# The last 48 rows of two expert tiles' down products, as four 64x64 products side by side

## The reference

```python
DIM = 256; INTER = 176; N_EXPERTS = 16; TOP_K = 2; N_SHARED = 2

def _swiglu(t, wa, wb, wo):
    h = jax.nn.silu(t @ wa.T) * (t @ wb.T)
    return h @ wo.T

t = x.reshape(-1, DIM)                       # 2048 tokens
scores = jax.nn.softmax(t @ gate_w.T, axis=-1)
weights, indices = jax.lax.top_k(scores, TOP_K)
y = jnp.zeros_like(t)
for e in range(N_EXPERTS):
    w_e = jnp.sum(jnp.where(indices == e, weights, 0.0), axis=-1)
    y = y + _swiglu(t, w1[e], w3[e], w2[e]) * w_e[:, None]
z = _swiglu(t, sw1, sw3, sw2)                # the shared experts, inner size 352
return (y + z).reshape(shape)
```

## Time and profile before

| | us |
|---|---|
| median of 3 runs | 681.43 |
| profiled execution | 684.4 |
| its span | 682.6 |
| PE busy | 608.7 (89%) |
| DVE busy | 527.3 (77%) |
| ACT busy | 517.4 (76%) |
| POOL busy | 427.4 (63%) |
| L1476, up products of the expert tiles, each column half | 59.5 and 59.6 |
| L1142, staging of down weights, 40 | 23.1 |

### The profile page before, as it was taken

The page is one execution under the profiler, slowest core; times in us unless marked ns, Lnnn a source line. Parts: engine busy times, 40 slices in busy tenths (PEclk is TensorE's granted clock), DMA queues, the critical chain, the costliest instruction groups (busy, mean ns, idle before and its releaser), DMA issues.

```text
span 682.6 us, 12684 instructions
## 1 busy us (share of the span) xinstructions
PE 608.7 (89%) x4476; PEld 498.8 (73%) x4479; DVE 527.3 (77%) x899; ACT 517.4 (76%) x1182; POOL 427.4 (63%) x261
## 2 busy tenths in 40 slices
PE   5799999999994698899999999899998787879993
PEld 3388999999993445799999999887774443445662
DVE  6898999999997899899999999878534543444464
ACT  3999999999995988999999999865454442333435
POOL 0028999999997004799999999920224465455402
PEclk8979999999996999999999999999999988898997
DMA  7022333333320000344444444461111122122163
GB/s 191 6 64 82 111 112 112 111 103 111 111 82 1 1 4 21 103 153 153 155 148 150 152 154 154 137 202 61 56 48 61 63 73 83 63 77 64 54 262 123
DMA packets 41595, 67.76 MB, mean 99 GB/s; under 512 B 6688, under 2 KB 20928, under 8 KB 41536
## 3 DMA queue, kind: packets, MB, share of 16 engines
q1 hardware_dynamic: 37696, 56.50, 25.7%
q0 software_dynamic: 3840, 10.49, 4.8%
HBM read 57.28 MB, written 9.70 MB: 98 GB/s over the span
## 4 chain that ended last, share of the span: by engine, by line
ACT 44%; PE 24%; DVE 12%; POOL 11%; issue 3%; another core or an unknown queue 2%; DMA 2%; DVEq 1%; POOLq 0%; ACTq 0%; SPq 0%
ACT rings L1045 20%; POOL arena L1184 9%; PE both L1476 8%; ACT rings L1033 8%; ACT late L1033 8%; PE bank L1483 4%; PE both L1463 4%; DVE st L443 1%; POOL residual L1194 1%; ACT tok_a L923 1%; ACT rings L923 1%; PE bank L1584 1%; ACT tok_a L996 1%; DVE rings L866 1%
## 5 line engine op out<-in xcount | busy, mean ns | idle before, releaser
L1184 POOL TENSOR_TENSOR arena<-arena,rings 128x1024 f32<-128x1024 f32 x126 | 296.3, 2372 | 13.3 <-DVE arena L658 8.7
L1383 PE MATMUL both<-rings,tok_a 128*128 128x128 f32 x1152 | 171.7, 278 | 3.7 <-DVE arena L658 2.9
L1383 PEld LDWEIGHTS both<-rings,tok_a 128*128 128x128 f32 x1152 | 148.6, 191 | 7.8 <-ACT rings L1045 3.6
L658 DVE TENSOR_TENSOR_SCAN arena<-rings,both 128x1024 f32<-128x1024 f32 x64 | 143.7, 2275 | 9.4 <-ACT rings L1033 6.4
L658 DVE TENSOR_TENSOR_SCAN arena<-late,both 128x1024 f32<-128x1024 f32 x62 | 139.3, 2274 | 8.2 <-ACT late L1033 6.5
L1412 PE MATMUL bank<-ident,arena 128*128 128x128 f32 x1024 | 133.0, 273 | 3.5 <-POOL arena L1184 2.3
L1412 PEld LDWEIGHTS bank<-ident,arena 128*128 128x128 f32 x1024 | 115.6, 141 | 4.6 <-POOL arena L1184 2.7
L1045 ACT ACTIVATE rings<-tok_a,b_tok 128x256 f32<-128x256 f32 x224 | 104.3, 515 | 0.0
L1045 ACT ACTIVATE rings<-ident,b_tok 128x128 f32<-128x128 f32 x288 | 99.1, 408 | 0.3
L1385 PE MATMUL both<-ident,rings 128*128 128x128 f32 x448 | 90.7, 273 | 0.0
L1476 PE MATMUL both<-w_sb,rings 128*64 x160 | 59.5, 521 | 18.1 <-DVE rings L804 16.4
(11 more groups left out here) (233 smaller groups left out, 1073.1 us busy)
## 6 DMA issues: line engine op xcount, KB each, us to landing
rings<-c_rows SPq DMA_DIRECT2D x128, 256.0 KB, 3.3
w_sb<-w SPq DMA_DIRECT2D x18, 352.0 KB, 4.1
arena<-w SPq DMA_DIRECT2D x2, 2048.0 KB, 12.6
residual<-x SPq DMA_DIRECT2D x4, 512.0 KB, 5.7
x_rows<-tok_a SPq DMA_DIRECT2D x4, 512.0 KB, 2.6
tok_a<-y_tok SPq DMA_DIRECT2D x4, 512.0 KB, 6.5
w_sb<-y_tok SPq DMA_DIRECT2D x4, 512.0 KB, 7.2
out<-residual SPq DMA_DIRECT2D x8, 256.0 KB, 2.6
```

Source lines behind the costliest of these rows:

```text
L658: dve.tensor_tensor_scan(h_s, decay_s.rearrange("p h t -> p (h t)"), both[s % B_RING][:, :], 0.0, ALU.mult, ALU.add).then_inc(h_ready, 1)
L1184: pool.tensor_tensor(h_both, h_both, c_row, ALU.mult).then_inc(hc_ready, 1)
L1383: pe.matmul(o, tok_a[:, c, h * P:(h + 1) * P], v_ring[:, s % V_RING, j, 0:P], start=True, stop=True)
```

## The change

The rows 0 to 127 of the contraction are done as before, by `down_main`: two products for each tile. The last 48 rows are done behind them for both tiles at once, by `down_rest`: the features of the even tile lie on partitions 0 to 47, those of the odd tile on 64 to 111, and each of the four products (tile by half) contracts over 64 partitions and has 64 token columns. `ty_ready` of both tiles is sent from there. So that the weights are on both halves of the partitions, the host lays the last 48 rows of `w2` twice, each padded to 64; the array keeps its size of 256 rows. The weights of the first half are now staged too, by the new `stage_rest` on ScalarE: 64 partitions and 256 values for each tile, with a register load, into a part of `feat_a` that is free by then. TensorE waits for them (`rest_staged`) ahead of the odd tile's main products. `turn` transposes features 64 to 175 of the odd tile in its second transpose (112 in place of 48), so that its last 48 come out on partitions 64 to 111.

```diff
+        staged_rest = feat_a[:, 0, 0:D]
...
             def turned_out(k):
 
                 act.activation(gatedT[:, k, 0, :], bank[2 + k][:, 0:P], ACT.Copy)
-                return act.activation(gatedT[0:IR, k, 3, :], bank[2 + k][0:IR, P:2 * P], ACT.Copy)
+                r = slice(k * UNIT, k * UNIT + IR)
+                return act.activation(gatedT[r, 0, 3, :], bank[2 + k][r, P:2 * P], ACT.Copy)
...
+            def stage_rest(at, i):
+
+                act.reg_load(first_reg[i % LOADS], half_e[0][0:1, at.slice(i)])
+                e = act.snap(first_reg[i % LOADS], min_val=0, max_val=E - 1)
+                r = slice(i % 2 * UNIT, (i % 2 + 1) * UNIT)
+                act.activation(staged_rest[r, :].unsqueeze(1), w2b[r, bass.ds(e, 1), :], ACT.Copy).then_inc(rest_staged, 1)
+
             def pair_step(at, j):
...
                     for i in (2 * j, 2 * j + 1):
                         stage_down(at, i)
+                    for i in (2 * j, 2 * j + 1):
+                        stage_rest(at, i)
...
             def turn(k):
                 pe.transpose(bank[2 + k][:, 0:P], gated[:, k, 0:P], ident[:, :])
-                return pe.transpose(bank[2 + k][0:IR, P:2 * P], gated[:, k, P:INTER], ident[:, :])
+                lo = P - k * UNIT
+                return pe.transpose(bank[2 + k][0:INTER - lo, P:2 * P], gated[:, k, lo:INTER], ident[:, :])
...
-            def down_halves(e, k):
-
-                for a in range(2):
-                    for t, w in zip(token_halves, ((w2a, w2b)[a][:, e, :], staged_down[:, k, a])):
-                        ins = pe.matmul(ysum[k][t, 0:D], gatedT[:, k, 3 * a, t], w, start=a == 0, stop=a == 1)
+            def down_main(e, k):
+
+                for t, w in zip(token_halves, (w2a[:, e, :], staged_down[:, k, 0])):
+                    pe.matmul(ysum[k][t, 0:D], gatedT[:, k, 0, t], w, start=True, stop=False)
+
+            def down_rest(k):
+
+                r = token_halves[k]
+                for t, w in zip(token_halves, (staged_rest[r, :], staged_down[r, k, 1])):
+                    ins = pe.matmul(ysum[k][t, 0:D], gatedT[r, 0, 3, t], w, start=False, stop=True)
                 return ins
...
                     pe.wait_ge(tgT_copied, at(i + 1))
                     pe.wait_ge(down_staged, at(i + 1))
-                    down_halves(bass.ds(expert(i), 1), i % 2).then_inc(ty_ready, 1)
+                    if i % 2:
+                        pe.wait_ge(rest_staged, at(i + 1))
+                    down_main(bass.ds(expert(i), 1), i % 2)
+                for i in (2 * j, 2 * j + 1):
+                    down_rest(i % 2).then_inc(ty_ready, 1)
...
+    w2 = i["L1_ffn_w2"].transpose(0, 2, 1)
...
-        "w13": np.concatenate([w1, w3], axis=1).transpose(0, 2, 1), "w2": np.pad(i["L1_ffn_w2"].transpose(0, 2, 1), ((0, 0), (0, 2 * P - INTER), (0, 0))),
+        "w13": np.concatenate([w1, w3], axis=1).transpose(0, 2, 1), "w2": np.concatenate([np.pad(w, ((0, 0), (0, UNIT - IR), (0, 0))) for w in (w2[:, 0:P + IR], w2[:, P:P + IR])], axis=1),
```

More of the change, by code:

```diff
@@ L241, in sandwich_kernel @@
         units_in, units_turned = sem("units_in"), sem("units_turned")
-        up_staged, down_staged = sem("up_staged"), sem("down_staged")
+        up_staged, down_staged, rest_staged = sem("up_staged"), sem("down_staged"), sem("rest_staged")
         rows_stored = sem("rows_stored")
@@ L1130, in turned_out @@
                 act.activation(gatedT[:, k, 0, :], bank[2 + k][:, 0:P], ACT.Copy)
-                return act.activation(gatedT[0:IR, k, 3, :], bank[2 + k][0:IR, P:2 * P], ACT.Copy)
+                r = slice(k * UNIT, k * UNIT + IR)
+                return act.activation(gatedT[r, 0, 3, :], bank[2 + k][r, P:2 * P], ACT.Copy)
             second_reg = [act.alloc_register(f"second_down{k}") for k in range(LOADS)]
+            first_reg = [act.alloc_register(f"first_down{k}") for k in range(LOADS)]
             def stage_down(at, i):
```

## The result

The changed kernel takes 674.55 us (median of five runs, 671.53 to 675.28), the kernel before 681.43 (five runs, 680.50 to 684.25): ratio 0.9874, 95% interval 0.9844 to 0.9904. The change makes it 6.9 us faster; the forecast was 2.9, at 678.6. The profiled execution took 674.55 us with a span of 672.7, against 684.4 and 682.6.

The account below looks back on a forecast made before the run. With gathers, GpSimd's runs of four transfers and TensorE's late signals pace steps; behind them TensorE does. Second regime -0.5, later run starts +1.0, one long wait less -3.4: -2.9, from 681.43 to 678.6 us; range 673 to 687.

Parts of the forecast that it names:

- TensorE's down part: TensorE's down products for a pair of tiles: 1.49 us in place of 1.83, 0.33 less a step.
- When the sums are ready: Even sum 0.53 us later, odd 0.33 earlier; VectorE's even copy just covered, so TensorE's 0.33 comes through.
- covered, cost nothing: ScalarE's two new copies, 0.7 us together, end before TensorE wants them; cost nothing, without that cover up to 0.2 a step.
- The end: Last pair: the end waits for the even sum's scatter, 0.53 us later against TensorE's start, +0.5.
- second regime: Stretch from 627 to 647 us, GpSimd only scattering, TensorE with hardly a gap: -1.0, with the last pair's +0.5 together -0.5.
- The start of GpSimd's run: Gather stretch: where the even sum's signal is on time and GpSimd empty, its run starts 0.5 later, twice: +1.0.
- The long waits: Gather stretch: VectorE's four waits of about 3.8 us for row transposes, 3.4 each; one of four less, -3.4.
- Most long waits go: Rival, gather stretch: three long waits go, -10.2 + 0.5, or the whole 0.33 arrives, -5.4; put at 674, chance 0.17.
- Run later and slower: Rival, gather stretch: the even sum's later copy delays GpSimd's run, one more long wait; +5, 686, chance 0.23.
- No overlap of the four products: Rival, TensorE: the last part takes four slots, +0.10 a step, even sum 0.96 later; +3.3, 684.7, chance 0.10.

Follow-up runs that it names:

- prompt chip: Kernels timed unedited on the kind of chip where the kernel before takes 655 to 658 us; changed kernel against it 1.0012 and, on another such chip, 1.0001.
- held chip: Kind of chip where the kernel before takes 681 to 688 us and TensorE's signals come late; changed kernel against it where first timed 0.9874.

## Why the prediction was right in sign and wrong in size

*TensorE's down part.* Right in kind: forecast 1.49 us, measured 1.56, so 0.27 saved in the place of 0.33. Four products side by side in two slots, starts 10 ns apart; the first of the two slots is 0.26 long (619.45 to 619.71) and not 0.216, and the way back to the full array costs 0.33 (619.71 to 620.04), so 0.59 for this group where 0.53 was taken.

*When the sums are ready, and ScalarE.* "It is just covered, so TensorE's 0.33 comes through" failed. The even sum's copy was to start 0.08 us ahead of the row transposes and starts 0.21 behind them (620.25 against 620.04), with the rows' copies queued behind it. The prediction took a sum to be ready at the end of its last slot, 0.22 us behind the slot's start; the copy, which waited for nothing else, starts 0.54 us behind that start (619.71). The new copies were sized at 0.36 each and are 0.42 (0.84 for two), but "covered, cost nothing" missed their place: they push the silus into each other, and with them VectorE's gates (0.54 us of waiting at 624.12). Behind the gathers 0.17 of the 0.33 us arrive in a step (5.13 for 5.30); in the loop on a prompt chip, where the chain shows both engines on it, none of it (5.30 and 5.31).

*The end.* Forecast -0.5 for the whole second regime; from the last gather to the last scatter it is +0.2.

*The start of GpSimd's run.* Forecast +1.0 for two late starts. Neither is there; the run starts 1.5 to 1.7 us behind the last in every step, since the sums are released with everything else. The reading that in ordinary steps what TensorE saves is not waited for was right, and the steps of 6.5 us stayed.

*The long waits.* This is the term that was mis-sized, and the step of the prediction that failed. "I expect fewer, and take one of four less, -3.4": all four went, and the gather stretch shrank by 13.6 us. That this is just the prediction's bound for all four, 4 x 3.4, is luck. The price was read from one step of the kernel before, "the slower products behind it included". Held against the same steps of the changed kernel, the four pairs of a short and a long step gave 2.3, 2.0, 3.3 and 3.3 us, 11.0 together; the other 2.6 came mostly from the steps of 7.1, 7.7 and 6.9 us behind them. In the two pairs that gave 2.3 and 2.0 TensorE ran at 2.4 GHz throughout; the two of 3.3 have the low clock in them. So a part of the price was the clock. The first of the two runs with the new copies early has four long steps too (9.4, 9.4, 9.0 and 8.6 us), with TensorE at 2.4 GHz throughout, and takes 106.3 us from the first scatter to the last gather, against 98.5 in the changed kernel and 112.0 in the one before. By these three executions, one of each kernel, the long waits are worth some 8 us, and most of the rest goes with the low clock.

The mechanism was the right one. The long wait needs the even sum's signal to slip through and that of the row transposes to be held; the change narrowed the time between the two by the odd tile's products, and doing only that, in the kernel before, gave the whole ratio (0.9868 against 0.9874). Why all four went where I took one is not shown. The count of long waits does not move as a whole: there are four in the kernel before, none in the changed one, two with hardly any new copies, four with the copies early. The last two both altered ScalarE alone, so what ScalarE does is part of it, and the change's own copies there may have helped; that is argued from these two runs, and the one that moved the odd tile's copy alone, also on ScalarE, has no long wait. Likewise argued: that the phase of TensorE against GpSimd repeats step for step once no signal slips through, as the uniform steps of 6.35 to 6.55 us suggest.

*The rivals.* "Most long waits go" was what happened, at 674 us, with a chance of 0.17. Run later and slower: only where VectorE's order was altered too. No overlap of the four products: not so.

*Sum.* By spans -13.6 + 0.2 for the stage and +3.5 elsewhere make -9.9; by the medians it is -6.9, since the profiled execution before was 3.0 us above its own median (the changed kernel's is at its median).

What stays open: what it is that holds TensorE's signals on a held chip. It is seen in the first timing and on three chips, with the gathers and not behind them, and never on the two prompt ones with the same instructions; a kernel without gathers was not run on a held chip, and whether one chip can be of both kinds was not seen.

## What to carry to other kernels

When the steps of a loop alternate short and long, ask what makes a step leave the common rhythm, and price a long one from several of its kind, with the clock beside each: here one was worth 2.0 us and another 3.3. An edit at that place may take more of them than it seems to, and a later edit elsewhere can bring some back. Where two signals of one engine are sent at different times and their receiver takes them in another engine's order, try sending them together before saving any work: on the held chip where it was tried, that alone gave the whole gain, for three lines. And an engine's saving comes through only if what it releases is released no later than before; the sum that is ready 0.3 us later stood at the head of VectorE's queue, and took the 0.3 us back.

No version tried beats the changed kernel on the held chips. On the prompt ones no version beats the kernel before by more than can be measured.

## What the runs showed of the hardware

- The same kernel took 681 to 688 us where it was first timed and on three chips, and 655 to 658 on two, 4% apart. The difference lies in the gather stretch, where most steps are 6.5 us and more against 5.3.
- On the held chips those signals of TensorE that fall around the last transfer of GpSimd's run of four come 0.9 to 1.0 us behind its end, five of them within 0.17 us; those of the up products, in the middle of the run, come within 0.04 us of the modelled end in the run with the signals together (in the changed kernel the odd tile's were 0.5 to 0.7 us late in eight steps of fifteen). On the prompt chips GpSimd issues indirect transfers 1.3 us apart without a pause, and all of TensorE's signals come in time.
- In the kernel before, TensorE's clock fell to 1.2 GHz for 6.8 us within an idle time of 3.75 us (to 575.92) and within one of 3.65 us (to 613.46), and for 3.4 us at 547.5 and 591.9, with no idle time over 1.6 us in the 20 us ahead of the first of these. In the changed kernel it waits 1.1 to 1.6 us in every step and stays at 2.4 GHz (1.00 from 519 to 617 us).
- Four fp32 products of 64x64 ran side by side, starts within 0.02 us; from their first slot to the second it was 0.26 us, and 0.33 from there to the row transposes, as against 0.216 and 0.32 for two of 128x64. A change of shape cost 0.10 us where one stood alone, and 0.15 where every group of two slots changed it. The Trainium skill ("TensorEngine Tiling (Array Packing)", section Key Properties) has a change of mode drain the engine, and this agrees.
